# Cross attention and a mixture of 12 experts on one core: the second expert layer of 12 of 16 tiles computed only for the rows routed to each expert

## The chip, the cores and the metric

The program runs on one core of a Trainium2 chip. The metric is device time in microseconds (us) of one execution. A core has five engines that run apart from each other and wait on semaphores: TensorE (PE, matrix products into the accumulation memory PSUM), VectorE (DVE), ScalarE (ACT), GpSimd (POOL) and SyncE (SP, which here issues transfers only).

## The reference, cut to what matters

```python
x = x + xattn(layernorm(x), ctx, mask)          # (2, 1024, 256), 16 heads, 64 keys
x = x + ffn(layernorm(x))

def ffn(x):                                     # 2048 rows of 256
    xa = x @ P_w.T                              # 64 wide
    C1, C2, C3 = (route(xa, U) for U in (U1, U2, U3))   # (2048, 12), three weights not zero in a row
    h = gelu(mixture(x, C1, W1))                # W1, W2: 12 matrices of 256 x 256
    return mixture(h, C2, W2) + C3 @ b2

def route(xa, U):                               # top 3 of 12, softmax over the three
    topv, topi = top_k(xa @ U.T, 3)
    return zeros.at[rows, topi].add(softmax(topv))

def mixture(inp, C, W):
    return sum(C[:, e:e+1] * (inp @ W[e].T) for e in range(12))
```

Only three of the twelve terms of a row are not zero.

## The kernel before, in words

The 2048 rows are 16 tiles of 128 rows (T = 16), held in `x_all`. A first part runs the attention tile by tile, with the transfers and the splitting of the expert weights beside it. A second part is the two expert layers. Both compute all twelve experts for every row and let a weight of zero drop a product. Experts come in pairs: one product of a tile with a pair is 128 x 512 in one bank of PSUM, and `split_product` (L931 to L937) makes it from six matmuls, three for each half of the 256 inputs: the high parts of both operands, and each high part with the other's low part. A layer of a tile, called a slot here, is six pairs or 36 matmuls of 512 columns. There are 32 slots.

For each expert VectorE then adds weight times product to one of two running sums (`sum_pair`, L820 to L833; L827 starts a sum, L832 goes on with it), twelve for a slot, and adds the two sums (`last_sum`, L837). ScalarE makes gelu (L580), the copies of the transposed tiles and their high parts (L502, L503, L570). VectorE makes the low parts (L763, L768), the statistics of the second layernorm (L604 to L607) and its result `xf` (L626), the three best of twelve logits (`find_top`, L774 to L785) and the weights (`combine_weights`, L791 to L810). GpSimd makes the inverse deviation (`inverse_deviation2`, L366 and L368) and the exponentials (L418), and splits the weights of the third routing (`split_c3`). SyncE stores a tile once its last sum is there.

The order of the work on each engine is written out by hand, and each engine takes its own in order. In `experts(t)` layer 1 of tile t + 1 comes before layer 2 of tile t, with the next tile's logits, transposes and routing between the pairs; this is a hardware loop over t from 1 to T - 3, with straight code before and behind it. A product's bank is written again once the sums of the slot before have read it (semaphore `acc`).

## Time and profile before

| what | value |
|---|---|
| three timed runs | 409.34, 409.06, 407.38 us; median 409.06 |
| the profiled execution | 410.84 us, its span 409.1 us |
| PE busy | 393.3 us, 96% of the span |
| DVE busy | 340.5 us, 83% |
| ACT, POOL busy | 112.9 us (28%), 111.4 us (27%) |
| chain that ended last | PE 83% (line L936 alone 66%), ACT 4%, DVE 4%, issue 4% |
| PE clock | 9 tenths or more of full speed in 38 of the 40 slices of the page |

The span is the profiled part of one execution, and 1.74 us lie around it. Busy is the sum of an engine's instruction times. Matmuls are pipelined, so that a matmul of 512 columns shows about 0.39 us busy while the next starts some 0.23 us behind it; times between starts are what counts. The page's row on PE's clock is in tenths of full speed.

### The profile page before, as it was taken

Reading aid. Unit: us, or ns where it says so; the run is one execution under the profiler, and the core shown is the slowest. Engines: PE = TensorE matmul, PEld = TensorE weight load, DVE = VectorE, ACT = ScalarE, POOL = GpSimd, SP = SyncE. Lnnn points to the kernel's source line nnn. Section 1 sums busy time; section 2 is a strip of 40 time slices with the busy share of each in tenths; the row PEclk is TensorE's granted clock in tenths of the full one; section 3 lists DMA queues with packets and bytes.
Section 4 is the critical chain, followed back from the end, with each engine's and each line's share of the span. In section 5 each row is a group of like instructions: output and inputs, shape, how many; then the busy total and the mean of one; then the engine's idle time right before and its main releaser. Section 6 shows DMA issues by size and latency. Waiting matters only on the chain.

```text
span 409.1 us, 7666 instructions
## 1 busy us (share of the span) xinstructions
PE 393.3 (96%) x2132; PEld 334.5 (82%) x2132; DVE 340.5 (83%) x1038; ACT 112.9 (28%) x261; POOL 111.4 (27%) x165
## 2 busy tenths in 40 slices
PE   4889999999999999999999999999999999999996
PEld 3679889898988888888888888888888888888884
DVE  4788898998885889789898888989789898888875
ACT  2477888888932101010000100001010000100000
POOL 5264556465540211202112020211202112020200
PEclk9989999999989999999999999999999999999999
DMA  7900131322000000000000000000000000000000
GB/s 233 330 2 2 52 103 53 102 78 76 2 0 2 2 0 15 13 0 13 0 13 13 0 13 0 13 0 13 13 0 13 0 13 12 1 13 0 14 0 26
DMA packets 8613, 12.72 MB, mean 31 GB/s; under 512 B 1076, under 2 KB 5016, under 8 KB 8472
## 3 DMA queue, kind: packets, MB, share of 16 engines
q1 hardware_dynamic: 8040, 12.44, 9.2%
q10 hardware_dynamic: 560, 0.13, 0.1%
q8 instruction: 6, 0.10, 0.1%
q14 instruction: 7, 0.06, 0.0%
HBM read 10.47 MB, written 2.10 MB: 31 GB/s over the span
## 4 chain that ended last, share of the span: by engine, by line
PE 83%; ACT 4%; DVE 4%; issue 4%; POOL 2%; DMA 1%; ACTq 0%; POOLq 0%; DVEq 0%; SPq 0%
PE banks L936 66%; PE banks L978 2%; PE banks L1003 2%; PE banks L1013 2%; PE banks L988 2%; PE banks L991 1%; PE banks L1053 1%; PE banks L993 1%; ACT w_h L543 1%; DVE q_hl L637 1%; POOL w_l L377 1%; ACT prob L480 1%; PE banks L1061 1%; PE banks L1043 1%; DMA x_all<-in_x_dram 1%
## 5 line engine op out<-in xcount | busy, mean ns | idle before, releaser
L832 DVE SCALAR_TENSOR_TENSOR s_d<-banks,c_cur,s_d 128x256 f32<-128x256 f32 x165 | 72.7, 479 | 25.3 <-PE banks L936 22.2
L936 PE MATMUL banks<-w_h,xf_h 128*128 128x512 f32 x204 | 81.4, 399 | 0.0
L936 PE MATMUL banks<-w_l,xf_h 128*128 128x512 f32 x204 | 80.0, 392 | 0.0
L936 PE MATMUL banks<-w_h,xf_l 128*128 128x512 f32 x204 | 79.7, 391 | 0.0
L418 POOL TENSOR_TENSOR top_e<-euler,top_d 128x9 f32<-128x9 f32 x16 | 29.0, 1813 | 181.5 <-DVE top_d L782 181.5
L936 PE MATMUL banks<-w_h,h_h 128*128 128x512 f32 x180 | 73.0, 405 | 0.0
L936 PE MATMUL banks<-w_l,h_h 128*128 128x512 f32 x180 | 70.5, 391 | 0.0
L936 PE MATMUL banks<-w_h,h_l 128*128 128x512 f32 x180 | 70.1, 389 | 0.0
L832 DVE SCALAR_TENSOR_TENSOR sum<-banks,c_new,sum 128x256 f32<-128x256 f32 x160 | 66.3, 479 | 2.8 <-PE banks L936 2.7
L570 ACT ACTIVATE h_h<-banks 128x256 fp32r<-128x256 f32 x15 | 5.8, 386 | 156.4 <-PE banks L1061 156.4
L936 PEld LDWEIGHTS banks<-w_l,xf_h 128*128 128x128 f32 x204 | 38.4, 188 | 8.3
L936 PEld LDWEIGHTS banks<-w_h,xf_l 128*128 128x128 f32 x204 | 38.7, 190 | 7.4
L936 PEld LDWEIGHTS banks<-w_h,xf_h 128*128 128x128 f32 x204 | 38.6, 189 | 7.4
L936 PEld LDWEIGHTS banks<-w_l,h_h 128*128 128x128 f32 x180 | 33.8, 188 | 7.6
L936 PEld LDWEIGHTS banks<-w_h,h_l 128*128 128x128 f32 x180 | 33.9, 188 | 6.3
L936 PEld LDWEIGHTS banks<-w_h,h_h 128*128 128x128 f32 x180 | 33.8, 188 | 6.0
L377 POOL TENSOR_TENSOR w_l<-stage,w_h 128x1024 f32 (+1 forms) x12 | 28.7, 2391 | 32.0 <-ACT w_h L543 32.0
L1013 PE MATMUL banks<-v_ext,prob_t 128*128 128x34 f32 x256 | 30.1, 273 | 0.2 <-ACT prob_t L488 0.2
L1013 PEld LDWEIGHTS banks<-v_ext,prob_t 128*128 128x128 f32 x256 | 29.9, 192 | 0.4 <-issue 0.4
L580 ACT ACTIVATE xn_t<-xn 128x256 f32<-128x256 f32 x16 | 6.7, 420 | 77.3 <-DVE xn L837 77.3
L643 DVE TENSOR_REDUCE s_max<-banks 128x16 f32<-128x1024 f32 x16 | 19.5, 1221 | 6.3 <-PE banks L993 6.3
L488 ACT ACTIVATE prob_t<-banks 128x512 f32<-128x512 f32 x32 | 17.5, 594 | 17.1 <-PE banks L1003 17.1
(129 smaller groups left out, 628.3 us busy)
## 6 DMA issues: line engine op xcount, KB each, us to landing
stage<-in_w_t_dram SPq DMA_DIRECT2D x12, 512.0 KB, 3.6
out_dram<-x_all SPq DMA_DIRECT2D x16, 128.0 KB, 1.9
x_all<-in_x_dram SPq DMA_DIRECT2D x1, 1024.0 KB, 7.8
x_all<-in_x_dram SPq DMA_DIRECT2D x1, 768.0 KB, 8.0
mask_all<-in_mask_dram SPq DMA_DIRECT2D x2, 256.0 KB, 5.2
wk_sb<-in_wk_t_dram SPq DMA_DIRECT2D x1, 256.0 KB, 3.0
x_all<-in_x_dram SPq DMA_DIRECT2D x2, 128.0 KB, 3.8
wq_sb<-in_wq_t_dram SPq DMA_DIRECT2D x1, 256.0 KB, 4.3
```

The source lines that it names most:

```text
L377: pool.tensor_tensor(w_l[:, n, :, :], stage[:, slot, :, :], w_h[:, n, :, :].bitcast(F32), ALU.subtract).then_inc(w_split, 1)
L418: pool.tensor_tensor(top_e[:, :], euler[:, :], top_d[:, :, :].rearrange("p r k -> p (r k)"), ALU.pow).then_inc(e_ready, 1)
L488: nc.scalar.activation(prob_t[:, j:j + HP // 2, :], ps_pt[:, j:j + HP // 2, :], ACT.Copy).then_inc(pt_copied, 1)
L570: nc.scalar.activation(h_buffers(t)[0][:, :, :], ps_t, ACT.Copy).then_inc(h_hi, 1)
L580: nc.scalar.activation(h[:, :], h_in[:, :], ACT.Gelu).then_inc(h_ready, 1)
L643: dve.tensor_reduce(s_max[:, :], ps_s, AX_X, ALU.max).then_inc(s_maxed, 1)
L832: dve.scalar_tensor_tensor(out=sums[e % 2][:, :], in0=product, scalar=weights[:, e:e + 1], in1=sums[e % 2][:, :], op0=ALU.mult, op1=ALU.ad ...
L936: ins = pe.matmul(dst, a(c), b(c), start=(i == 0), stop=(i == len(terms) - 1))
L978: ins = pe.matmul(ps_q[:, m, :], wq_sb[:, c, m * P:(m + 1) * P], xn_t[:, c, :], start=(c == 0), stop=(c == C - 1))
L988: pe.matmul(banks[:, c, :].rearrange("p (h k) -> p h k", k=KEYS), ident_b[:, :], mask_bias[:, t, :].unsqueeze(1).to_broadcast([P, HPC, KEY ...
L1003: ins = pe.transpose(ps_pt[:, j, :], prob[:, 2 * j:2 * j + 2, :].rearrange("p h k -> p (h k)"), ident[:, :])
L1013: ins = pe.matmul(ps_v[:, j * 2 * VW:(j + 1) * 2 * VW], prob_t[:, j, :], v_ext[:, b, j, :], start=True, stop=True)
```

## The change: what it does

The first layer stays dense for all 16 tiles, and so does the second for the last four. For tiles 0 to 11 (S = 12) layer 2 is done from lists.

First phase, tiles 0 to 12 of layer 1 alone. For each of tiles 0 to 11 ScalarE writes gelu's result three times, each time scaled with the weight of one of the row's three choices (`weigh_h`), and GpSimd scatters the three with indirect DMAs (`send_h`) to `h_rows` in DRAM. There each expert owns a region of 13 x 128 rows. The row's place in the list comes from two small matmuls that count the rows chosen so far (`rank`) and three VectorE instructions (`rows_of`). The sums of the first pair of experts, the result of the layernorm and the copy of the logits go from VectorE to ScalarE (`first_pair`, `normalise2`, `copy_z`).

Between the phases VectorE works out a table of blocks (`table_ends`, `table_blocks`), and SyncE writes 128 rows of zeros behind the end of each of the twelve lists, at a row number that it loads from the table.

Second phase, 47 blocks of 128 rows. SyncE loads a block of `h_rows` at a row number from the table, up to eight ahead; TensorE transposes it, ScalarE and VectorE make its high and low part, TensorE multiplies it with the 256 x 256 matrix of one expert, whose offset it loads from the table, and ScalarE copies the product to a buffer that SyncE stores to `y_rows`. In the same phase the bias of tiles 0 to 11 is added to `x_all`.

Third phase, the four dense tiles as before. Beside them GpSimd fetches the results back with 36 indirect DMAs that add into `x_all`, three for each of the twelve tiles, each behind the one before it on the same tile. The loops of the expert part are now written out.

```diff
+    S = 12
+    REGION = (S + 1) * P
+    ZERO_ROW = EXPERTS * REGION
+    BLOCKS = (S * P * TOP_K + EXPERTS * (P - 1) + EXPERTS - TOP_K) // P
+    assert REGION % P == 0 and (REGION // P) * EXPERTS <= 256
...
+        h_rows = nc.dram_tensor("h_rows", (ZERO_ROW + P, D), F32)
+        y_rows = nc.dram_tensor("y_rows", (BLOCKS * P, D), F32)
...
-            def store(b, j, sums):
-                sp.wait_ge(acc, sums)
-                sp.dma_start(out_dram[:, b, j, :], x_all[:, j + b * TPB, :]).then_inc(stored, 16)
-            for b in range(BATCH):
-                with sp.Fori(0, TPB if b < BATCH - 1 else TPB - 1) as j:
-                    store(b, j, 2 * SUMS * j + (2 * SUMS * b * TPB + 3 * SUMS))
-            store(BATCH - 1, TPB - 1, 2 * SUMS * T)
+            sp.wait_ge(zeros_set, 1)
+            sp.dma_start(h_rows[ZERO_ROW:ZERO_ROW + P, :], zero_rows).then_inc(tails_set[0], 16)
+            sp.wait_ge(table, 2)
+            for e in range(EXPERTS):
+                row = sp.value_load(end_row[0:1, e:e + 1], min_val=e * REGION, max_val=e * REGION + S * P)
+                sp.dma_start(h_rows[bass.ds(row, P), :], zero_rows).then_inc(tails_set[e * ZEROS // EXPERTS], 16)
+            def load_block(j):
+                row = sp.value_load(block_row[j:j + 1, 0:1], min_val=0, max_val=ZERO_ROW)
+                if j >= LOADS:
+                    sp.wait_ge(block_t, j - LOADS + 1)
+                sp.dma_start(h_in_block[j % LOADS], h_rows[bass.ds(row, P), :]).then_inc(block_in[j % LOADS], 16)
+            sp.wait_ge(table, TABLE)
+            for i in range(2):
+                sp.wait_ge(h_sent[i], 16 * TOP_K * S // 2)
+            for i in range(ZEROS):
+                sp.wait_ge(tails_set[i], 16 * EXPERTS // ZEROS + (16 if i == 0 else 0))
+            for j in range(LOADS):
+                load_block(j)
+            for j in range(BLOCKS):
+                sp.wait_ge(block_out, j + 1)
+                sp.dma_start(y_rows[j * P:(j + 1) * P, :], y_block[j % STORES]).then_inc(y_sent[j % STORES], 16)
+                if j + LOADS < BLOCKS:
+                    load_block(j + LOADS)
+            def store(t):
+                sp.dma_start(out_dram[:, t // TPB, t % TPB, :], x_all[:, t, :]).then_inc(stored, 16)
+            for t in range(S):
+                sp.wait_ge(y_back[t], 16 * TOP_K)
+                store(t)
+            for t in range(S, T):
+                sp.wait_ge(acc, SUMS * slot2(t) + SUMS)
+                store(t)
             sp.wait_ge(stored, 16 * T)
...
+                if t >= 2:
+                    pool.wait_ge(xf_ready, t)
                 pool.tensor_tensor(rstd2[:, :], var_eps2[:, :], minus_half[:, :], ALU.pow).then_inc(rstd2_ready, 1)
+                if t >= 2:
+                    pool.wait_ge(rstd2_ready, t + 1)
+                    pool.tensor_scalar(shift2[:, :], mean_var2[:, 0:1], rstd2[:, 0:1], -1.0,
+                                       ALU.mult, ALU.mult).then_inc(shift2_ready, 1)
...
+            def send_h(t):
+                pool.wait_ge(row_set, t + 1)
+                pool.wait_ge(h_weighed, TOP_K * (t + 1))
+                for k in range(TOP_K):
+                    pool.indirect_dma_start(out=h_rows[:, :], out_offset=bass.IndirectOffsetOnAxis(h_row[:, t, k:k + 1], 0),
+                                            in_=h_w[t % 2][k], in_offset=None).then_inc(h_sent[t % 2], 16)
+            def fetch_y(t, k):
+                if k > 0:
+                    pool.wait_ge(y_back[t], 16 * k)
+                else:
+                    pool.wait_ge(y_added, t + 1)
+                pool.indirect_dma_start(out=x_all[:, t, :], out_offset=None, in_=y_rows[:, :],
+                                        in_offset=bass.IndirectOffsetOnAxis(y_row[:, t, k:k + 1], 0),
+                                        compute_op=ALU.add).then_inc(y_back[t], 16)
             exponentials(0)
             inverse_deviation2(1)
             exponentials(1)
-            split_c3(0)
-            with pool.Fori(2, T) as t:
-                inverse_deviation2(t)
-                exponentials(t)
-                split_c3(t - 1)
-            split_c3(T - 1)
+            inverse_deviation2(2)
+            for t in range(1, S + 1):
+                send_h(t - 1)
+                if t < S:
+                    inverse_deviation2(t + 2)
+                    exponentials(t + 1)
+            exponentials(S + 1)
+            for t in range(S + 1):
+                split_c3(t)
+            inverse_deviation2(S + 2)
+            fetches = [(g + i, k) for g in range(0, S, 4) for k in range(TOP_K) for i in range(4)]
+            pool.wait_ge(y_step, 4)
+            for i in range(STORES):
+                pool.wait_ge(y_sent[i], 16 * len(range(i, BLOCKS, STORES)))
+            for t, k in fetches[0:8]:
+                fetch_y(t, k)
+            split_c3(S + 1)
+            exponentials(S + 2)
+            inverse_deviation2(S + 3)
+            for t, k in fetches[8:20]:
+                fetch_y(t, k)
+            exponentials(S + 3)
+            split_c3(S + 2)
+            for t, k in fetches[20:]:
+                fetch_y(t, k)
+            split_c3(S + 3)
...
+            def weigh_h(t):
+                act.wait_ge(h_ready, t + 1)
+                if t >= 2:
+                    act.wait_ge(h_sent[t % 2], 16 * TOP_K * (t // 2))
+                for k in range(TOP_K):
+                    nc.scalar.activation(h_w[t % 2][k], h[:, :], ACT.Copy,
+                                         scale=w_all[:, t, 1, k:k + 1]).then_inc(h_weighed, 1)
+            def first_pair(t):
+                act.wait_ge(route, ROUTE_STEPS * (t + 1))
+                act.wait_ge(acc, SUMS * slot1(t))
+                act.wait_ge(pair_done, PAIRS * slot1(t) + 1)
+                for e in range(2):
+                    nc.scalar.activation(sum1[e][:, :], banks[:, BANK[0], e * D:(e + 1) * D], ACT.Copy,
+                                         scale=c_all[:, t, 0, e:e + 1]).then_inc(acc, 1)
+            def normalise2(t):
+                act.wait_ge(xft_done, t)
+                act.wait_ge(shift2_ready, t - 1)
+                nc.scalar.activation(xf[:, :], x_all[:, t, :], ACT.Identity, bias=shift2[:, 0:1],
+                                     scale=rstd2[:, 0:1]).then_inc(xf_ready, 1)
+            normalise2(2)
+            for t in range(1, S + 1):
+                gelu(t - 1)
+                weigh_h(t - 1)
+                first_pair(t)
+                copy_xf(t + 1)
+                if t < S:
+                    normalise2(t + 2)
+                copy_z(t + 1)
+            def block_high(j):
+                act.wait_ge(block_t, j + 1)
+                if j >= HT:
+                    act.wait_ge(block_done, j - HT + 1)
+                nc.scalar.activation(bt_h[j % HT], banks[:, j % HT, 0:D].rearrange("p (c t) -> p c t", c=C),
+                                     ACT.Copy).then_inc(block_hi, 1)
+            def block_copy(j):
+                act.wait_ge(block_done, j + 1)
+                if j >= STORES:
+                    act.wait_ge(y_sent[j % STORES], 16 * (j // STORES))
+                nc.scalar.activation(y_block[j % STORES], banks[:, Y_BANK[j % HT], 0:D], ACT.Copy).then_inc(block_out, 1)
+            gelu(S)
+            block_high(0)
+            block_high(1)
+            for j in range(BLOCKS):
+                if j + 2 < BLOCKS:
+                    block_high(j + 2)
+                if j % 3 == 2 and 1 <= j // 3 <= S:
+                    copy_c3t(j // 3 - 1)
+                block_copy(j)
...
+            def rows_of(t):
+                dve.wait_ge(rank_done, t + 1)
+                dve.tensor_tensor(at_rank[:, :, :], at_e[:, 1, :, :],
+                                  ps_rank.unsqueeze(2).to_broadcast([P, EXPERTS, TOP_K]), ALU.mult).then_inc(rank_used, 1)
+                if t < S - 1:
+                    with nc.allow_low_precision(reason="whole numbers up to 256"):
+                        dve.tensor_tensor(taken[:, :], taken[:, :], picked[:, :], ALU.add).then_inc(taken_set, 1)
+                dve.wait_ge(rank_used, t + 1)
+                with nc.allow_low_precision(reason="whole numbers, as integers"):
+                    dve.tensor_reduce(h_row[:, t, :], at_rank[:, :, :].rearrange("p e k -> p k e"), AX_X,
+                                      ALU.add).then_inc(row_set, 1)
...
+            for t in range(1, S + 1):
+                layer1_pairs(t, range(1, 2))
+                xf_low(t + 1)
+                layer1_pairs(t, range(2, 3))
+                if t < S:
+                    stats2(t + 2)
+                else:
+                    table_blocks()
+                layer1_pairs(t, range(3, 4))
+                if t < S:
+                    find_top(t + 1)
+                layer1_pairs(t, range(4, PAIRS))
+                if t < S:
+                    rows_of(t)
+                    if t == S - 1:
+                        table_ends()
+                    combine_weights(t + 1)
+            def block_low(j):
+                dve.wait_ge(block_hi, j + 1)
+                dve.tensor_tensor(bt_l[j % HT], banks[:, j % HT, 0:D].rearrange("p (c t) -> p c t", c=C),
+                                  bt_h[j % HT].bitcast(F32), ALU.subtract).then_inc(block_lo, 1)
+            def add_bias(t):
+                dve.wait_ge(y_done, t + 1)
+                dve.tensor_tensor(x_all[:, t, :], ps_y, x_all[:, t, :], ALU.add).then_inc(y_added, 1)
+            for j in range(BLOCKS):
+                block_low(j)
+                if j == 2:
+                    find_top(S + 1)
+                if j == 5:
+                    combine_weights(S + 1)
+                if 6 <= j < 10:
+                    rows_of_y(j - 6)
+                if j % 3 == 1 and 2 <= j // 3 <= S + 1:
+                    add_bias(j // 3 - 2)
...
+            def transpose_block(j):
+                pe.wait_ge(block_in[j % LOADS], 16 * (j // LOADS) + 16)
+                if j < HT:
+                    pe.wait_ge(acc, SUMS * S + 2 * j + 2)
+                else:
+                    pe.wait_ge(block_lo, j - HT + 1)
+                for c in range(C):
+                    ins = pe.transpose(banks[:, j % HT, c * P:(c + 1) * P], h_in_block[j % LOADS][:, c * P:(c + 1) * P],
+                                       ident[:, :])
+                ins.then_inc(block_t, 1)
+            def multiply_block(j):
+                start = pe.value_load(block_w[j:j + 1, 0:1], min_val=0, max_val=(PAIRS - 1) * 2 * C * D + D)
+                pe.wait_ge(block_lo, j + 1)
+                if j < HT:
+                    pe.wait_ge(acc, SUMS * S + 2 * (j + HT) + 2)
+                else:
+                    pe.wait_ge(block_out, j - HT + 1)
+                part = lambda w: lambda c: w[:, bass.ds(start + c * 2 * D, D)]
+                split_product(banks[:, Y_BANK[j % HT], 0:D], (lambda c: bt_h[j % HT][:, c, :], lambda c: bt_l[j % HT][:, c, :]),
+                              (part(w2_h), part(w2_l))).then_inc(block_done, 1)
+            pe.wait_ge(table, TABLE)
+            transpose_block(0)
+            transpose_block(1)
+            for j in range(BLOCKS):
+                if j + 2 < BLOCKS:
+                    transpose_block(j + 2)
+                multiply_block(j)
+                if j % 3 == 2 and 1 <= j // 3 <= S:
+                    expert_bias(j // 3 - 1)
+                if j % 3 == 1 and 1 <= j // 3 <= S:
+                    transpose_c3(j // 3 - 1)
+            pe.wait_ge(block_lo, BLOCKS)```

What SyncE does in the expert part before is this loop, run for the first eight tiles (`x_all` is a tile, `out_dram` the output):

```order
18 L318 UNCONDITIONAL_BRANCH
19 L318 ISA
20 L315 ISA [waits acc]
21 L315 DMA out_dram<-x_all 128x256
22 L318 REGISTER_ALU
23 L318 COMPARE_AND_BRANCH
```

And this is SyncE now in the second phase, two blocks of it (`prob` is a buffer of results, `bo_sb` holds the table, `stage` is a buffer of loaded blocks):

```order
99 L405 DMA y_rows<-prob 128x256 [waits block_out]
100 L391 TENSOR_LOAD bo_sb
101 L391 ISA x2
102 L394 ISA [waits block_t]
103 L394 DMA stage<-h_rows 128x256
104 L405 DMA y_rows<-prob 128x256 [waits block_out]
105 L391 TENSOR_LOAD bo_sb
106 L391 ISA x2
107 L394 ISA [waits block_t]
108 L394 DMA stage<-h_rows 128x256
```

A block has two transfers where a tile had one, and one load of a register from a table. The twelve writes of zeros stand ahead in the same form, each with its own load and one transfer.

ScalarE before, one turn of the loop of the expert part (`xn_t` is gelu's result, `h_h`, `xf_h` the high parts, `c_t` the transposed weights):

```order
150 L570 ACTIVATE h_h<-banks 128x256 [waits ht_done]
151 L574 ACTIVATE c_t<-banks 96x128 [waits c3t_done]
152 L577 REGISTER_ALU
153 L580 ACTIVATE xn_t<-xn 128x256 [waits ht_done,acc]
154 L499 REGISTER_ALU
155 L501 REGISTER_ALU [waits xft_done]
156 L502 ACTIVATE xf_t<-banks 128x256 [waits z_done]
157 L503 ACTIVATE xf_h<-banks 128x256
```

ScalarE now, one tile of the first phase (`prob_t` and `s_d` are the weighed copies, `sum_0` and `sum_1` the running sums, `xf` the result of the layernorm, `z_sb` the logits):

```order
226 L754 ACTIVATE xn_t<-xn 128x256 [waits h_weighed,acc]
227 L762 ACTIVATE prob_t<-xn_t,mask_all 128x256 [waits h_sent1,h_ready]
228 L762 ACTIVATE s_d<-xn_t,mask_all 128x256 x2
229 L771 ACTIVATE sum_0<-banks,mask_all 128x256 [waits pair_done,acc,route]
230 L771 ACTIVATE sum_1<-banks,mask_all 128x256
231 L666 ACTIVATE xf_t<-banks 128x256 [waits z_done,xft_done]
232 L667 ACTIVATE xf_h<-banks 128x256
233 L777 ACTIVATE xf<-x_all,shift,rstd 128x256 [waits shift2_ready,xft_done]
234 L673 ACTIVATE z_sb<-banks 128x36 [waits route,z_done]
```

The logits' copy stands behind the layernorm's result of the tile after, which waits for GpSimd's `shift2`.

GpSimd before, one turn of its loop:

```order
90 L366 TENSOR_TENSOR var_eps<-mean_var,eps 128x1 [waits stats2_ready]
91 L368 TENSOR_TENSOR rstd<-var_eps,minus_half 128x1 [waits var2_ready]
92 L417 ISA
93 L418 TENSOR_TENSOR top_e<-euler,top_d 128x9 [waits route]
94 L428 REGISTER_ALU [waits c_moved]
95 L429 TENSOR_TENSOR c_hlh<-c_cur,ones 128x2x12 [waits c3t_done]
96 L434 TENSOR_TENSOR c_hlh<-c_cur,c_hlh 128x12 [waits c3_hi]
```

GpSimd now, one tile of the first phase:

```order
118 L567 DMA h_rows<-prob_t,mask_all 20096x256 [waits h_weighed,row_set]
119 L567 DMA h_rows<-s_d,mask_all 20096x256 x2
120 L463 TENSOR_TENSOR var_eps<-mean_var,eps 128x1 [waits stats2_ready]
121 L467 TENSOR_TENSOR rstd<-var_eps,minus_half 128x1 [waits xf_ready,var2_ready]
122 L470 TENSOR_SCALAR shift<-mean_var,rstd 128x1 [waits rstd2_ready]
123 L546 TENSOR_TENSOR top_e<-euler,top_d 128x9 [waits route]
```

Three indirect DMAs now stand ahead of the inverse deviation, and one instruction more makes `shift2`.

## Rows read from the trace of the kernel before

**Rows 1.** Busy time by stretch: start:end, length, PE, PEld, DVE, ACT, POOL, clock, DMA

```profile
116.00:118.00 2.00, 1.03 (x5) 1.04 (x6) 1.92 (x15) 1.06 (x1) 0.35 (x1) 0.65 0.00 0
118.00:120.00 2.00, 2.00 (x7) 1.71 (x7) 1.62 (x8) 0.00 (x0) 1.92 (x3) 0.50 0.00 0
...
174.00:300.00 126.00, 126.00 (x589) 104.63 (x588) 108.97 (x374) 10.65 (x36) 21.01 (x36) 1.00 0.02 7
```

**Rows 2.** The chain that ended last: start, length, what

```profile
147.42 8.29 PE banks L936 x36
...
164.98 8.29 PE banks L936 x36
...
397.24 8.20 PE banks L936 x36
405.46 0.89 DVE s_d L832 x2
```

**Rows 3.** VectorE in order of time, start and length first, experts begin

```profile
133.99 0.20 DVE L774 COPY z_sb<-banks 128x36 f32<-128x36 f32 x1
...
137.60 0.27 DVE L810 TENSOR_REDUCE c_new<-w_at_e 128x36 f32<-128x108 f32 x1
```

**Rows 4.** VectorE in order of time, one turn of the loop

```profile
176.30 2.44 DVE L832 SCALAR_TENSOR_TENSOR sum<-banks,c_new,sum 128x256 f32<-128x256 f32 x6
178.77 0.42 DVE L837 TENSOR_TENSOR xn<-sum,sum 128x256 f32<-128x256 f32 x1
...
185.15 0.17 DVE L778 MAX8 top<-z_sb 128x8 f32<-128x12 f32 x1
...
186.01 1.74 DVE L832 SCALAR_TENSOR_TENSOR s_d<-banks,c_cur,s_d 128x256 f32<-128x256 f32 x4
...
188.34 0.27 DVE L791 TENSOR_TENSOR at_e<-top_i,iota_e 128x108 f32<-128x108 uint32 x1
...
190.02 0.43 DVE L604 BATCH_NORM_STATS2 bn<-x_all 128x6 f32 x1 [0.29 <-issue]
190.50 0.18 DVE L607 BATCH_NORM_AGGREGATE mean_var<-bn 128x2 f32<-128x6 f32 x1
...
190.81 0.88 DVE L827 TENSOR_SCALAR sum<-banks,c_new 128x256 f32<-128x256 f32 x2
```

**Rows 5.** ScalarE in order of time, same turn

```profile
179.23 0.42 ACT L580 ACTIVATE xn_t<-xn 128x256 f32<-128x256 f32 x1 [5.16 <-DVE xn L837]
179.55 0.37 ACT L502 ACTIVATE xf_t<-banks 128x256 f32<-128x256 f32 x1
```

**Rows 6.** GpSimd in order of time, same turn

```profile
185.75 1.80 POOL L418 TENSOR_TENSOR top_e<-euler,top_d 128x9 f32<-128x9 f32 x1 [11.71 <-DVE top_d L782]
...
190.75 0.19 POOL L366 TENSOR_TENSOR var_eps<-mean_var,eps 128x1 f32<-128x1 f32 x1 [1.65 <-DVE mean_var L607]
191.02 0.54 POOL L368 TENSOR_TENSOR rstd<-var_eps,minus_half 128x1 f32<-128x1 f32 x1
```

**Rows 7.** SyncE's issues of transfers in order of time

```profile
0.80 0.44 SPq L290 DMA_DIRECT2D wk_sb<-in_wk_t_dram  x1
1.30 0.45 SPq L291 DMA_DIRECT2D x_all<-in_x_dram  x1
```

**Rows 8.** Transfers by line, KB of one, median us from issue to landing

```profile
out_dram<-x_all SPq DMA_DIRECT2D x16, 128.0 KB, 1.9
```

**Rows 9.** TensorE in order of time: 256 columns at either clock, transposes

```profile
104.53 0.28 PE L936 MATMUL banks<-wo_h,a_h 128*128 128x256 f32 x1
104.64 0.28 PE L936 MATMUL banks<-wo_h,a_l 128*128 128x256 f32 x1
...
117.56 0.41 PE L936 MATMUL banks<-wo_l,a_h 128*128 128x256 f32 x1
117.77 0.41 PE L936 MATMUL banks<-wo_h,a_h 128*128 128x256 f32 x1
...
177.68 0.38 PE L1043 MATMUL banks<-ident,xf 128*128 128x128 f32 x2
177.81 0.48 PE L936 MATMUL banks<-w_h,h_h 128*128 128x512 f32 x1
```

364 lines of the change are left out of this document (267 added, 97 removed).

## The prediction

> **What bounds the kernel now.** I read the page's busy shares first (PE 96%), then the busy time by stretch: from 174 to 300 us TensorE is busy in all of 126 us at full clock, VectorE in 109 of them, ScalarE in 11 [rows 1]. The chain of waits gives the pace: the same piece of 36 matmuls comes again after 164.98 - 147.42 = 17.56 us, which is two slots, 8.78 us each [rows 2]. So each slot taken away is worth 8.78 us, as long as TensorE stays the bound, and layer 2 of twelve tiles is 12 x 8.78 = 105.4 us. The other engines' order of time then tells what bounds each new phase; in all three phases I find that it is another engine than TensorE for some or all of the time.
>
> **First phase, layer 1 of tiles 1 to 12.** It starts where the weights of tile 1 are ready, 137.9 us in the trace [rows 3]; one set of statistics comes ahead of that (0.79) and two small copies go (about 0.2 each), so 138.4.
> TensorE needs about 8.8 us for a tile. VectorE, by rows 4: ten sums at 2.47/6 = 0.41 (from 176.30 to 178.77), 4.1; the last sum and the low part, 0.42 each, 0.84; statistics 190.81 - 190.02 = 0.79; the three best 186.01 - 185.15 = 0.86; the weights 190.02 - 0.29 - 188.34 = 1.4 and one more small reduction, 0.15; three small instructions for the list places, about 0.5. Sum 8.6, as much as TensorE. What tips it are two waits that the new order makes.
> The first: the second pair waits for ScalarE's first pair, which waits for the weights that VectorE has just made. Two ScalarE instructions, 179.55 - 179.23 = 0.32 and 0.42 [rows 5], and two hand-overs of 0.04 give 0.8. Gelu and its three weighed copies stand ahead of it, but 4 x 0.32 = 1.3 fit beside the list places and the weights (2.0).
> The second: the three best of tile t + 1 wait for the copy of the logits, which stands behind the layernorm's result of tile t + 2, which waits for GpSimd. From the end of the aggregate (190.68) GpSimd has the inverse deviation at 191.56, 0.88 later [rows 4, 6]; then `shift2` about 0.25, two ScalarE instructions 0.6, hand-overs 0.1: 1.8. VectorE has one pair (0.82) in that time: a wait of 1.0. Queued behind it on VectorE are the last two pairs, whose banks TensorE needs.
> So a tile takes 8.6 + 0.8 + 1.0 = 10.4 us instead of 8.8. Eleven of them lead to 138.4 + 114.4 = 252.8, and the list ends (0.6) to 253.4.
> GpSimd's three scatters stand ahead of the inverse deviation. No row shows an indirect DMA. From below one costs an issue on SyncE, 0.5 [rows 7], from above the longest GpSimd instruction here, 1.8 [rows 6]. I take 1.2, the middle, as neither row is near. Three are 3.6 us, begun 0.6 before the weights are done, so ended 3.0 after; the statistics are ended 3.5 after. At 1.2 they hide, at 1.8 they cost about 1.5 us a tile.
>
> **Between the phases.** SyncE starts the twelve writes of zeros at about 252. Each is a load of a register, three register instructions and an issue. Issues follow each other at 1.30 - 0.80 = 0.50, and the gap in it is 0.06, which I take as the price of a register instruction (0.15 for three) [rows 7]. A register load from a table no row shows. Below it is such a gap, 0.05; above, the shortest way to memory and back, 1.9 us [rows 8]. I take 0.5, the price of the nearest thing that SyncE itself carries out, an issue. Twelve times 1.15 is 13.8; with 1.9 to land the first block is loaded from 252 + 13.8 + 1.9 = 267.7. Layer 1 of tile 12 ends at about 262, so TensorE is idle for some 8 us with the first load's landing.
> The Trainium skill ("DMA: Bandwidth & Descriptors", section "Latency and other measured facts") gives such a load a floor of about 600 ns; 0.1 us more 59 times would make the end 6 us later, some 425 us.
>
> **Second phase, 47 blocks.** TensorE: two transposes 177.81 - 177.68 = 0.13 and six matmuls of 256 columns at 0.11 to 0.12 [rows 9], 0.85 with the bias now and then. ScalarE: two instructions, 0.8. VectorE: one, 0.42. SyncE: a store 0.5, a register load 0.5, three register instructions 0.15, a load 0.5: 1.65 us a block. SyncE takes its queue in order, so prefetching eight blocks doesn't help; it is the slowest, and bounds. 47 x 1.15 + 39 x 0.5 = 73.6 to the issue of the last load: 341.3. Landing 1.9, and that block's transposes, high part, low part, product and hand-overs, 2.3: 345.5. TensorE has a register load of its own for each block, 0.5 on its sequencer, beside matmuls already queued: hidden under 1.65.
> When TensorE waits, its clock falls: after a stretch in which it was busy for half of 2 us the granted clock is 0.50, that is 1.2 GHz, and matmuls of 256 columns come every 0.21 us [rows 1, 9]. A block is then 6 x 0.21 + 0.26 = 1.5 us, still under SyncE's 1.65. It costs nothing here, but is a floor for the fast rival below. The Trainium skill warns of this ("TensorE: Matmul & The Clock Gate", section "Why this matters for your kernels": gaps between bursts take the clock back to half). By that rule no cheap register load saves more than 0.15 us a block.
>
> **Third phase.** Seven dense slots: three turns of 17.56 and 8.2 [rows 2], 60.9 us. Some 2 us more for a slow clock at its start. Beside them GpSimd has 36 fetches of 1.2, 43.2 us, and between them the exponentials of tiles 14 and 15 and `split_c3` of 13 to 15. Played through: fetches start 3 us in (the last store's 1.9 and its issue); eight take it to 12.6; exponentials (1.8) and the inverse deviation to 18.2, no later than wanted; twelve to 32.6; the exponentials of tile 15 end at 34.4, which delays its weights by about 1.2; sixteen fetches to 54.2, and only then comes `split_c3(15)`. TensorE wants its transpose 13.2 us into the third turn, at 48.3 + 1.2. It waits 5.4. Together 6.6 us; at 0.5 a fetch nothing, at 1.8 some 25. The end behind the last matmul is as before, 409.1 - 405.44 = 3.7.
>
> **The sum.** 345.5 + 60.9 + 2.0 + 6.6 + 3.7 = 418.7 us of span; with the 1.74 around it 420.4 in terms of the profiled execution (410.84). The median of the runs is 0.996 of that execution: 419 us. Set against each other: 105.4 go; 77.8 of blocks come (73.6 + 1.9 + 2.3), 18.4 of slower first phase (115.0 instead of 11 x 8.78), 5.5 of change-over (267.7 - 253.4, less the slot of tile 12), 8.6 in the third phase, and 4.7 in which TensorE's lead over VectorE at the start (it began tile 1 some 4 us before its weights were there) buys nothing more.
>
> **Rivals.**
> Cheap sequencers, faster (0.27). Register loads cost 0.15 and indirect DMAs under 0.9. The zeros land at 263.5, 47 blocks take 47 x 0.8 + 39 x 0.5 = 57, the third phase has no wait: about 391 us of span, 391 in the runs' terms; with the second wait of the first phase gone too, 382. If TensorE's half clock holds 1.5 us a block, 13 us come back, about 404. For it: the gap of 0.06 between issues says that SyncE is quick with simple things. Against: a register load has to read memory.
> Dear register loads, slower still (0.13). At 1.3 us each it is 59 x 0.8 = 47 us more: 466; at 1.9, 500. The sum crosses the 409 of before at about 0.33 us, with all else as above: from there the change is slower.
> Dear indirect DMAs, slower (0.12). At 1.8: 11 x 1.5 in the first phase and 18 in the third, about 453. For it: GpSimd builds 128 separate rows for each, and no row of this trace has anything of that kind.
> The change doesn't do what it says (0.01): the 47 blocks and their transfers all stand in the order of instructions, so that nothing speaks for it.
> My own case, SyncE bounding blocks at 1.4 to 2.0 us, has 0.47, and its own range is 405 to 440.
>
> **How the numbers follow.** A measurement of this kernel can tell about 0.5% (2 us) from no change. The fast rival gives nearly all of the chance of faster, 0.27, with a little of my own case's lower end, 0.28; its edge near 409 gives 0.05 for no change; the rest is slower, 0.67. The range of 387 to 460 leaves out the lowest of the fast rival and most of the dear register loads, one in ten each.
>
> **What would show it.** In the profile after: VectorE starts a new tile of the first phase every 10 to 11 us, with waits on ScalarE ahead of the second pair and of the three best; TensorE busy about 85% there. SyncE's issues in the second phase stand in pairs, 1.65 us a block, without waits for the blocks' semaphores; TensorE busy half of it or at half clock. In the third phase one wait of TensorE for `c3_hlh` of tile 15. Wrong would be: SyncE waiting for ScalarE's copies in the second phase (then TensorE or ScalarE bounds, and the time is 400 or less), tiles of the first phase at 9 us, or scatters that hold the inverse deviation up.

## The result, and the profile after

| | before | after |
|---|---|---|
| median of the runs | 409.2 us (407.38 to 409.44, 4 runs) | 459.76 us (458.69 to 461.17, 4 runs) |
| ratio | | 1.125, 95% interval 1.120 to 1.130 |
| span of the profiled execution | 409.1 us | 456.6 us |
| TensorE busy | 96% | 80% |

The change made the kernel 51 us slower. The prediction was 419 us, 10 us slower: the direction was right, the size was not, and the time lies at the very end of the range of 387 to 460, 20 us above the 405 to 440 of the prediction's own case. The page's shares and the by-engine line of its chain of waits say that no single engine bounds the kernel any more:

```profile
PE 366.2 (80%) x2078; PEld 303.8 (67%) x2078; DVE 278.3 (61%) x908; ACT 178.0 (39%) x439; POOL 208.9 (46%) x262
issue 23%; PE 21%; DVE 19%; POOL 17%; ACT 11%; SPq 5%; DMA 4%; POOLq 0%; DVEq 0%; ACTq 0%
```

Busy time by stretch, in the columns of [rows 1]: a piece of the first phase, the change-over, the blocks, the third phase.

```profile
174.00:262.00 88.00, 77.04 (x346) 60.42 (x347) 59.83 (x285) 29.46 (x80) 45.35 (x56) 0.94 0.11 37
264.00:283.00 19.00, 6.67 (x31) 4.98 (x31) 8.67 (x34) 3.67 (x10) 3.02 (x3) 0.78 0.33 111
300.00:350.00 50.00, 40.30 (x265) 33.20 (x265) 17.30 (x41) 22.44 (x71) 4.47 (x20) 0.97 0.51 159
364.00:457.00 93.00, 62.07 (x266) 50.28 (x264) 44.28 (x132) 7.09 (x22) 61.99 (x47) 0.84 0.43 74
```

Before, TensorE was busy in all of the 126 us of [rows 1]. Now it is idle for 12% of the first phase, two thirds of the change-over and a third of the third phase, and its granted clock is lower in each, at its lowest where it is idle most.

**First phase.** VectorE in order of time, one tile (before: [rows 4]). Between the weights of tile 5 and the three best of tile 6 stand two waits (the first row is the three best of the tile before, 11.20 us ahead of the last one, and that is the period):

```profile
193.70 0.17 DVE L1011 MAX8 top<-z_sb 128x8 f32<-128x12 f32 x1 [2.31 <-issue]
...
198.01 0.27 DVE L1047 TENSOR_REDUCE mask_all<-w_at_e 128x36 f32<-128x108 f32 x1
199.28 0.88 DVE L1074 SCALAR_TENSOR_TENSOR sum<-banks,mask_all,sum 128x256 f32<-128x256 f32 x2 [1.01 <-ACT sum L771]
...
201.65 0.18 DVE L839 BATCH_NORM_AGGREGATE mean_var<-bn 128x2 f32<-128x6 f32 x1
...
204.90 0.17 DVE L1011 MAX8 top<-z_sb 128x8 f32<-128x12 f32 x1 [2.30 <-issue]
```

GpSimd in the same tile (before: [rows 6]), where the scatters stand ahead of the inverse deviation:

```profile
199.25 1.06 POOL L567 DMA_INDIRECT h_rows<-prob_t,mask_all  x1 [3.13 <-ACT s_d L762]
200.62 0.96 POOL L567 DMA_INDIRECT h_rows<-s_d,mask_all  x1 [0.30 <-issue]
201.89 0.96 POOL L567 DMA_INDIRECT h_rows<-s_d,mask_all  x1 [0.30 <-issue]
202.87 0.20 POOL L463 TENSOR_TENSOR var_eps<-mean_var,eps 128x1 f32<-128x1 f32 x1
...
203.82 0.26 POOL L470 TENSOR_SCALAR shift<-mean_var,rstd 128x1 f32<-128x1 f32 x1
```

and ScalarE (before: [rows 5]), where the copy of the logits stands behind the normalisation:

```profile
197.57 0.90 ACT L762 ACTIVATE s_d<-xn_t,mask_all 128x256 f32<-128x256 f32 x2
...
204.18 0.60 ACT L777 ACTIVATE xf<-x_all,shift,rstd 128x256 f32<-128x256 f32 x1 [4.44 <-POOL shift L470]
204.68 0.18 ACT L673 ACTIVATE z_sb<-banks 128x36 f32<-128x36 f32 x1
```

The aggregate ends at 201.83, and GpSimd takes it up at 202.87. The wait of 2.30 is labelled "issue"; these three rows name it: the copy ends at 204.86, and VectorE goes on at 204.90.

**Change-over.** SyncE's issues (before: none of this kind; one issue is [rows 7]), with count and length of a run of them:

```profile
265.73 13.11 SPq L388 DMA_DIRECT2D h_rows<-wo_sb  x12
281.01 8.11 SPq L394 DMA_DIRECT2D stage<-h_rows  x8
289.16 0.43 SPq L405 DMA_DIRECT2D y_rows<-prob  x1
290.34 0.34 SPq L394 DMA_DIRECT2D stage<-h_rows  x1
290.72 0.43 SPq L405 DMA_DIRECT2D y_rows<-prob  x1
```

The last three are the blocks' pace, 290.72 - 289.16 = 1.56 us for a store and a load. The copies of the blocks' results, a row that sums up line 801 (count: least, median and greatest ns, first and last start), give 72.6 / 46 = 1.58:

```profile
L801 ACT ACTIVATE prob<-banks x47: 384/384/388, 288.2 to 360.8; 128x256 f32<-128x256 f32 x47
```

**Third phase.** GpSimd in order of time near its middle and end. There is nothing of the kind in the rows of before:

```profile
402.72 1.54 POOL L576 DMA_INDIRECT x_all<-y_rows,mask_all  x1 [0.30 <-issue]
404.57 1.54 POOL L576 DMA_INDIRECT x_all<-y_rows,mask_all  x1 [0.30 <-issue]
405.56 2.43 POOL L546 TENSOR_TENSOR top_e<-euler,top_d 128x9 f32<-128x9 f32 x1
...
436.52 1.55 POOL L576 DMA_INDIRECT x_all<-y_rows,mask_all  x1 [0.30 <-issue]
...
438.42 0.21 POOL L559 TENSOR_TENSOR c_hlh<-mask_all,c_hlh 128x12 f32<-128x12 f32 x1
```

One fetch starts 1.85 us behind the other. VectorE waits for the exponentials that stand behind them, and TensorE for the split of tile 15:

```profile
408.02 0.16 DVE L1030 TENSOR_REDUCE e_sum<-top_e 128x3 f32<-128x9 f32 x1 [10.54 <-POOL top_e L546]
```

```profile
438.69 0.45 PE L1407 MATMUL banks<-ident,c_hlh 128*96 128x128 f32 x1 [18.49 <-POOL c_hlh L559]
```

### The profile page after: what moved, and what is told of

The parts are those of the page before. It is cut to its first block, busy times and chain, and to the rows that moved or that the text cites. A ratio compares the mean times of both kernels' runs of the same rounds, so it can differ in the third digit from the quotient of the medians.

```text
span 456.6 us, 7680 instructions
## 1 busy us (share of the span) xinstructions
PE 366.2 (80%) x2078; PEld 303.8 (67%) x2078; DVE 278.3 (61%) x908; ACT 178.0 (39%) x439; POOL 208.9 (46%) x262
## 3 DMA queue, kind: packets, MB, share of 16 engines
q0 software_dynamic: 6912, 9.44, 10.4%
## 4 chain that ended last, share of the span: by engine, by line
issue 23%; PE 21%; DVE 19%; POOL 17%; ACT 11%; SPq 5%; DMA 4%; POOLq 0%; DVEq 0%; ACTq 0%
POOL x_all L576 11%; PE banks L1269 11%; DVE sum L1074 8%; DMA y_rows<-prob 3%; ACT prob L801 2%; ACT sum L771 2%; PE banks L1311 2%; PE banks L1336 2%; POOL top_e L546 2%; POOL w_l L480 2%; PE banks L1321 2%; SPq L387 1%; DVE q_hl L871 1%; DVE top_i L1018 1%; PE banks L1324 1%
## 5 line engine op out<-in xcount | busy, mean ns | idle before, releaser
L1074 DVE SCALAR_TENSOR_TENSOR sum<-banks,mask_all,sum 128x256 f32<-128x256 f32 x160 | 68.0, 475 | 28.0 <-ACT sum L771 14.9
L576 POOL DMA_INDIRECT x_all<-y_rows,mask_all x36 | 56.1, 1557 | 14.6 <-issue 10.4
L546 POOL TENSOR_TENSOR top_e<-euler,top_d 128x9 f32<-128x9 f32 x16 | 29.7, 1857 | 51.6 <-DVE top_d L1015 51.6
L1269 PE MATMUL banks<-w_h,h_h 128*128 128x512 f32 x120 | 52.2, 435 | 0.0
L1269 PE MATMUL banks<-w_h,xf_h 128*128 128x512 f32 x120 | 50.6, 422 | 0.0
L1269 PE MATMUL banks<-w_h,h_l 128*128 128x512 f32 x120 | 49.8, 415 | 0.0
L1269 PE MATMUL banks<-w_l,h_h 128*128 128x512 f32 x120 | 49.7, 414 | 0.0
L1269 PE MATMUL banks<-w_l,xf_h 128*128 128x512 f32 x120 | 48.5, 404 | 0.0
L1269 PE MATMUL banks<-w_h,xf_l 128*128 128x512 f32 x120 | 48.5, 404 | 0.0
L567 POOL DMA_INDIRECT h_rows<-prob_t,mask_all x24 | 24.5, 1021 | 42.8 <-ACT prob_t L762 20.4
L1269 PE MATMUL banks<-w_h,kbd_hh 128*128 x94 | 32.7, 348 | 12.7 <-ACT prob L801 9.2
L1074 DVE SCALAR_TENSOR_TENSOR s_d<-banks,mask_all,s_d 128x256 f32<-128x256 f32 x44 | 19.4, 479 | 28.2 <-PE banks L1269 27.7
L801 ACT ACTIVATE prob<-banks 128x256 f32<-128x256 f32 x47 | 18.1, 384 | 40.3 <-PE banks L1269 31.3
L777 ACT ACTIVATE xf<-x_all,shift,rstd 128x256 f32<-128x256 f32 x14 | 8.4, 602 | 54.8 <-POOL shift L470 54.8
## 6 DMA issues: line engine op xcount, KB each, us to landing
stage<-h_rows SPq DMA_DIRECT2D x47, 128.0 KB, 2.0
y_rows<-prob SPq DMA_DIRECT2D x47, 128.0 KB, 2.0
out_dram<-x_all SPq DMA_DIRECT2D x16, 128.0 KB, 2.3
h_rows<-wo_sb SPq DMA_DIRECT2D x13, 128.0 KB, 1.7
```

Of the source, the lines that this page charges most:

```text
L546: pool.tensor_tensor(top_e[:, :], euler[:, :], top_d[:, :, :].rearrange("p r k -> p (r k)"), ALU.pow).then_inc(e_ready, 1)
L567: pool.indirect_dma_start(out=h_rows[:, :], out_offset=bass.IndirectOffsetOnAxis(h_row[:, t, k:k + 1], 0), in_=h_w[t % 2][k], in_offset=No ...
L576: pool.indirect_dma_start(out=x_all[:, t, :], out_offset=None, in_=y_rows[:, :], in_offset=bass.IndirectOffsetOnAxis(y_row[:, t, k:k + 1], 0),
L801: nc.scalar.activation(y_block[j % STORES], banks[:, Y_BANK[j % HT], 0:D], ACT.Copy).then_inc(block_out, 1)
L1074: dve.scalar_tensor_tensor(out=sums[e % 2][:, :], in0=product, scalar=weights[:, e:e + 1], in1=sums[e % 2][:, :], op0=ALU.mult, op1=ALU.ad ...
L1269: ins = pe.matmul(dst, a(c), b(c), start=(i == 0), stop=(i == len(terms) - 1))
```

## The experiments

Every kernel below is the changed kernel (459.76 us) with the edit shown. The diffs give it in short. "Before" was 407 to 409 us beside each, and this difference between the rounds of runs means that 2 us or less between two kernels tell nothing. Pitch is the time from one block's result copy to the next, mean over all.

### First phase: the copy of the logits

```diff
-                if t < S:
-                    normalise2(t + 2)
                 copy_z(t + 1)
+                if t < S:
+                    normalise2(t + 2)
```

> One change in ScalarE's order in the first expert phase: the copy of the logits of tile t+1 stands ahead of the normalisation of tile t+2. Theory: the 2.30 us in which VectorE waits ahead of its MAX8 in every tile come from this copy standing behind the normalisation, which waits for the inverse deviation that GpSimd makes only between its scatters. Then that wait falls under 0.5, the tile period from 11.20 to 9.0 to 9.6 us, and the time from 460 to 436 to 443. Rival: the late inverse deviation is needed anyway and only moves the wait to TensorE's transposes or to the exponentials; then the period stays within 0.3 of 11.20 and the time within 3 us.

Measured: 435.22 us, 24.5 less. VectorE's rows:

```profile
184.18 0.17 DVE L1011 MAX8 top<-z_sb 128x8 f32<-128x12 f32 x1
...
193.00 0.17 DVE L1011 MAX8 top<-z_sb 128x8 f32<-128x12 f32 x1
```

and the busy time of the same kernel:

```profile
180.00:240.00 60.00, 60.00 (x295) 48.50 (x294) 50.91 (x240) 24.63 (x67) 39.33 (x49) 1.00 0.14 47
```

No wait stands ahead of the three best any more, and the period is 193.00 - 184.18 = 8.82, TensorE's slot of [rows 2]: a little better than the theory had it. The rival is out: GpSimd's inverse deviation still stands behind the scatters (it starts 1.04 us behind the statistics, as before), and it costs nothing here, since TensorE is busy in all of the 60 us.

### Change-over: the zeros

```diff
                 sp.dma_start(stage[...], w_dram[layer][...]).then_inc(w_in[n % RING], 16)
+                sp.dma_start(h_rows[n * REGION:n * REGION + 5 * P, :]..., zero_rows...).then_inc(tails_set, 16)
-            for e in range(EXPERTS):
-                row = sp.value_load(end_row[0:1, e:e + 1], ...)
-                sp.dma_start(h_rows[bass.ds(row, P), :], zero_rows)...
```

> The zeros that the table placed behind each expert's list between the first phase and the blocks (12 writes of 128 rows) are written early instead, at fixed rows: rows 0 to 639 of each expert's region, one write behind each of the 12 loads of expert weights, ahead of the first scatter. Theory: TensorE's 12.2 us of idle time before the blocks are SyncE's 12 issues with their register loads (13.1 us); without them the first block load is issued some 2 us behind the table, and 10 to 13 us go. Rival: the 7.9 MB of zeros delay the weight loads or the first scatters and give part of it back, so that less than 5 us goes.

Measured: 451.84 us, 7.9 less, under the expected 10 to 13. The first phase starts and ends 1.4 us later, so the early zeros cost that at most. The chain of waits shows what is late next (start, length, what):

```profile
270.46 2.42 DMA h_rows<-s_d,mask_all
272.97 0.47 SPq L390
273.95 0.36 SPq L393
```

and VectorE's last row of the table of blocks:

```profile
272.35 0.21 DVE L1173 TENSOR_SCALAR bo_sb<-wv_sb 128x1 int32<-128x1 f32 x1
```

The first load goes out at 273.95 instead of 281.01, and it could not go much earlier: the table is ready at 272.56, and tile 11's last scatter lands at 272.88. Both had been covered by the zeros. So the first load is 6.5 us behind the weights of tile 12 and not 14.9: 8.4 of the zeros' 13.1 us, less the 1.4 of the longer first part. The load is 1.4 us behind the table, as the theory wanted; its 10 to 13 us forgot that the table itself is made beside the zeros. These early zeros go to fixed rows, the first 640 of each expert's region (768 in x_best12 below), and not to the end of each list: as the edit stands, it holds only for inputs whose lists end there.

### Blocks: SyncE, TensorE or the copies

First SyncE's register loads alone:

```diff
-                row = sp.value_load(block_row[j:j + 1, 0:1], min_val=0, max_val=ZERO_ROW)
-                sp.dma_start(h_in_block[j % LOADS], h_rows[bass.ds(row, P), :])
+                sp.dma_start(h_in_block[j % LOADS], h_rows[fixed row:fixed row + P, :])
```

> SyncE's loads of the 47 blocks use fixed row numbers in place of a register loaded from the table, so the wrong rows are multiplied; the amount of data and the number of transfers stay. Theory: SyncE's own instructions set the block's 1.56 us, of which the register load is 0.65 to 0.7; without it SyncE needs 0.9 and TensorE's 1.0 to 1.2 bounds: 0.35 to 0.45 less for each of 39 blocks and 0.65 less for each of the 8 first loads, 16 to 23 us in all. Rival: the transfers (160 GB/s, 2 us of landing) or ScalarE's two copies bound the block, and less than 5 us goes.

Measured: 457.87 us, 1.9 less, pitch 1.54. The theory fell: SyncE isn't the only bound. It now waits for ScalarE's copies ahead of 44 of its 47 stores (22 before, 9.4 us in all, 37.1 now), so it has time to spare. TensorE's rows of this kernel show the other:

```profile
299.72 0.38 PE L1268 MATMUL banks<-w_h,kbd_hh 128*128 x1 [0.15 <-ACT prob L800]
...
300.54 0.38 PE L1548 MATMUL banks<-ident,stage 128*128 128x128 f32 x2
301.13 0.38 PE L1268 MATMUL banks<-w_h,kbd_hh 128*128 x1 [0.22 <-ACT prob L800]
...
302.84 0.38 PE L1268 MATMUL banks<-w_h,kbd_hh 128*128 x1 [0.41 <-ACT prob L800]
```

Ahead of each product stands a gap of 0.15 to 0.41, put down to ScalarE's `prob`. But that copy was long done, as the product needs only the one of three blocks ago. What also stands ahead of the product is TensorE's own register load. The next two kernels test this.

```diff
-                start = pe.value_load(block_w[j:j + 1, 0:1], ...)     (ahead of product j)
+                start = block_start(j + 1)                            (behind product j)
-                sp.dma_start(y_rows[j * P:(j + 1) * P, :], y_block[j % STORES])
+                act.dma_start(y_rows[j * P:(j + 2) * P, :]..., two blocks of prob_f)
```

> Two changes in the block loop together: TensorE loads the register for block j+1 right behind the product of block j (ahead of the transposes of block j+3), and the stores of the block results are issued by ScalarE, two blocks in one transfer, in place of SyncE. Theory: with fixed rows on SyncE the pitch fell only from 1.56 to about 1.47, since TensorE's own register load leaves a gap of 0.2 to 0.4 before each product; SyncE and TensorE are two bounds of nearly the same size. With both gone the pitch is 1.2 to 1.3 (ScalarE's two copies of 0.38 and half a store), 11 to 16 us less in all. Rival: the chain of ScalarE's copy, VectorE's subtraction and the three buffers bounds the loop, and less than 5 us goes, or stores on ScalarE's queue hold its copies and nothing goes.

Measured: 453.3 us, 6.5 less, pitch 1.44: half of what the theory gave.

```diff
-                return pe.value_load(block_w[j:j + 1, 0:1], ...)
+                return j // 8 * 2 * C * D + j // 4 % 2 * D
```

> The block loop of x_blocks (453.3 us, pitch 1.44), in which TensorE in addition takes its weights from fixed places in place of a register, so products use the wrong expert's weights; SyncE keeps its register loads. Theory: even behind the product TensorE's register load leaves some 0.37 ahead of the next transposes, and it is this that bounds the pitch; then it falls to 1.15 to 1.25, where ScalarE's copies and SyncE's load are next, and 9 to 13 us go from 453. Rival: the chain of transpose, ScalarE's copy, VectorE's subtraction bounds it (TensorE was seen waiting for VectorE in 16 of 40 blocks), and the pitch stays over 1.38, less than 3 us.

Measured: 445.19 us, 8.1 less than x_blocks, 1 us short of the expected range; the pitch is 57.6 / 46 = 1.25, as expected:

```profile
L799 ACT ACTIVATE prob<-banks x47: 381/383/391, 289.0 to 346.6; 128x256 f32<-128x256 f32 x47
```

So TensorE's register load costs 0.19 us a block even behind the product. With SyncE's register loads gone the block took 1.54; before, SyncE's issues filled 1.56 without a gap. These are two bounds of nearly one size, and taking one of them away shows almost nothing. SyncE's is read from its rows; no kernel took TensorE's away alone.

### Third phase: number, order and price of the fetches

```diff
-fetches = [(g + i, k) for g in range(0, S, 4) for k in range(TOP_K) for i in range(4)]
+fetches = [(g + i, k) for g in range(0, S, 4) for k in range(1) for i in range(4)]
```

> Of the 36 adding fetches only the first of three for each tile is left, 12 in all, so the outputs of two of three routed experts are left out for 12 tiles. Theory: GpSimd's 1.85 us per fetch holds up the small work that stands behind them (the weights' exponentials and the split of tile 15), 11 and 21 us of waiting. Then the third phase falls from 96 to about 67 us and the time to 428 to 434. Rival: the phase is held by TensorE's lower clock or by the dense slots themselves, and the fetches only lie beside them: then less than 5 us goes.

The small work between the fetches then stands behind the third and the seventh fetch, so that the order changes with the number. Measured: 429.16 us, 30.6 less. TensorE is busy in 57.58 of the 61 us from 364 to 425, at full clock. The rival is out.

```diff
-            for t, k in fetches[0:8]: ...
-            split_c3(S + 1); exponentials(S + 2); inverse_deviation2(S + 3)
-            for t, k in fetches[8:20]: ...
-            exponentials(S + 3); split_c3(S + 2)
-            for t, k in fetches[20:]: ...
-            split_c3(S + 3)
+            fetches[0:6]; split_c3(S + 1); exponentials(S + 2); fetches[6]; inverse_deviation2(S + 3)
+            fetches[7:12]; split_c3(S + 2); exponentials(S + 3)
+            fetches[12:16]; split_c3(S + 3); fetches[16:]
```

> All 36 fetches stay, but GpSimd's small work stands in the list where its inputs are ready: the split of tile 13 and the exponentials of tile 14 behind 6 fetches, the inverse deviation of tile 15 behind 7, the split of 14 and the exponentials of 15 behind 12, the split of 15 behind 16. Theory: the rate, not only the order, is the bound: TensorE ends some 30 us earlier, but GpSimd needs 36 x 1.85 = 66.6 and about 12 for the rest from 363.9 on, then 3.9 of landing and 2 of the store, so the end is near 449 instead of 456.6: 6 to 11 us less. Rival: order alone costs the time, and the end goes to where TensorE ends: 25 to 30 us less, as with 12 fetches.

Measured: 452.17 us, 7.6 less. VectorE's last row and GpSimd's:

```profile
425.52 0.42 DVE L1082 TENSOR_TENSOR x_all<-s_d 128x256 f32<-128x256 f32 x1
```

```profile
442.84 1.54 POOL L576 DMA_INDIRECT x_all<-y_rows,mask_all  x1 [0.30 <-issue]
```

Counted from the phase's first product (363.74 in this run), the dense tiles now end after 62.2 us, just as with twelve fetches; before this edit it was 454.2 - 360.6 = 93.6. Yet the kernel ends with the last fetch, its landing and its store. Order gives 8 us of the 31; the rest is the fetches' own time.

```diff
                 pool.indirect_dma_start(out=x_all[:, t, :], ..., in_offset=...y_row[:, t, k:k + 1]...,
-                                        compute_op=ALU.add)
+                                        )
```

> The 36 fetches write in place of adding, so the sum over a row's three experts and the residual are left out for 12 tiles; number, rows and order of the fetches stay. Theory: it is the adding that makes a fetch 1.54 us where a scatter is 1.02; then each falls to about 1.0 and the third phase ends 12 to 20 us earlier. Rival: a fetch by a list of rows costs this much with or without adding (1.54 stays), and less than 3 us goes.

Measured: 446.82 us, 12.9 less. The row of the fetches:

```profile
L576 POOL DMA_INDIRECT x_all<-y_rows,mask_all x36: 945/957/1061, 363.1 to 423.4; - x36
```

0.96 us instead of 1.55, so adding costs 0.59 us for each; without it a fetch costs what a scatter does (0.96). The pitch of plain ones is 1.26, near the 1.2 that the prediction took for all.

36 x 0.59 is 21 us, and only 12.9 came off. GpSimd, sooner done with its fetches, waits 10.1 us for the inputs of its small work, where it waited 1.9. In this kernel alone some waits are labelled "remote", VectorE's the longest (us, times, longest):

```profile
DVE s_d L1073 <- remote: 17.3, 4, 6.2
```

The wait of 6.2 stands ahead of the three best of tile 15, and with it come 3.7 of GpSimd's 10.1 us. ScalarE too copies the logits of tile 15 only at 396.11, some 5 us behind the matmuls that make them. What holds these engines up was not tested.

### How much to route, and the parts together

x_s10 changes only S (with GpSimd's small work placed between the fetches of each dense tile); x_best12 joins the copy of the logits, the early zeros, the block loop of x_blocks and the order of x_crit_first; x_best10 is the same with S = 10.

```diff
-    S = 12
+    S = 10
```

> Only the number of routed tiles goes from 12 to 10 (41 blocks, 30 fetches, 6 dense tiles), with GpSimd's small work of each dense tile placed between the fetches; none of the other repairs. Theory, from the durations of the changed kernel: two tiles less at 11.2 are 22.4, six blocks less at 1.58 are 9.5, the third phase goes from 96 to about 101, where TensorE is its bound: 459.8 - 22.4 - 9.5 + 5 = 433, between 428 and 438, still slower than before (408). Rival: the third phase is held by the fetches as before, 30 x 1.85 in the way of the dense tiles: over 445.

Measured: 432.19 us, as the sum of the durations had it (433). The rival is out: with thirty fetches, placed between the small work, TensorE is busy in 92.80 of the 94 us from 334 to 428.

> All repairs of x_best10 with 12 routed tiles as in the change (zeros written to rows 0 to 767). Theory: against 395.1 the first phase has 2 x 9.0 and the blocks 6 x 1.45 more, and GpSimd's 36 x 1.85 + 12 + landing and store (about 85 to 88 us) bound the third phase where 10 tiles needed 99.5: 395.1 + 18 + 8.7 - 13 = 409, between 405 and 413: repaired, the change as it was sized comes out even with the kernel before. Rival: the adding fetches lie beside TensorE's work as a whole, which needs only 66 us: 390 or less.

Measured: 411.16 us, ratio 1.005 (1.002 to 1.008), within the forecast: even with the kernel before, or slower by half a per cent. Its busy time in the third phase:

```profile
325.00:405.00 80.00, 57.72 (x268) 47.49 (x266) 44.48 (x132) 7.10 (x22) 62.26 (x47) 0.88 0.48 78
```

> All of these together, with 10 routed tiles in place of 12 (41 blocks, 30 fetches, 6 dense tiles): the logits' copy ahead of the normalisation, early zeros, TensorE's register loads ahead, stores on ScalarE's queue, and GpSimd's small work placed between the fetches, per dense tile. Theory: from 435.2 of the reordered copy, two tiles fewer take 2 x 9.0 and 6 x 1.56 from the first two phases, the third is bounded by TensorE again (66 + 2 x 17 = 100 us against 30 x 1.85 + some 15 on GpSimd): 412; less 12 for the blocks and 12 for the zeros: 388, between 380 and 396, so faster than the kernel without routing (408). Rival: TensorE's lower clock in the change-over and extra waits take the gains back: 400 to 412.

Measured: 395.09 us, ratio 0.970 (0.965 to 0.974): 3% faster than before, within the forecast but 7 us above its middle. Its third phase:

```profile
297.00:390.00 93.00, 92.18 (x429) 76.13 (x427) 70.82 (x224) 13.15 (x40) 60.11 (x53) 1.00 0.37 64
```

With twelve routed tiles GpSimd is the bound of this phase (62 of 80 us busy, before its gaps of 0.3), with ten TensorE is again, at full clock, and the fetches lie beside it.

```diff
-                if j + 1 < BLOCKS:
-                    start = block_start(j + 1)
+                if j % 4 == 3:
+                    starts = [block_start(i) for i in range(j + 1, min(j + 5, BLOCKS))]
```

> x_best10 with TensorE's register loads for four blocks in a row behind every fourth product. Theory: the time of a register load is mostly latency and four in a row overlap, so that the gap of 0.37 in each of 41 blocks falls to about 0.1: 8 to 11 us less than 395.1. Rival: loads run one after the other, four cost four times one and the longer gap isn't covered by a product: no gain, or up to 12 us more.

Measured: 406.46 us, 11.4 more than x_best10 (before was 1.6 higher in this round), pitch 65.5 / 40 = 1.64 instead of 1.45. TensorE's row behind one such group of four:

```profile
263.10 0.41 PE L1560 MATMUL banks<-ident,stage 128*128 128x128 f32 x2 [2.34 <-issue]
```

2.34 / 4 = 0.59 us a load. The rival was right: register loads in a row don't overlap.

## Why the prediction was wrong, point by point

The sum failed by 456.6 - 418.7 = 37.9 us of span. By its own milestones:

| milestone | predicted | measured | step, over |
|---|---|---|---|
| weights of tile 12 | 253.4 | 266.1 | 12.7 |
| first block load issued | 267.7 | 281.0 | 0.6 |
| product of the last block | 345.5 | 360.6 | 1.8 |
| end of the span | 418.7 | 456.6 | 22.8 |

**The term that failed is the price of an adding fetch.** The prediction said "no row shows an indirect DMA", set 0.5 and 1.8 as bounds and took 1.2 as the middle. It is 1.54 and a gap of 0.30, so 1.85 from start to start, above the upper bound: that row, a single GpSimd instruction, couldn't bound an instruction and the gap behind it. The mechanism was right, and was written down as the rival "dear indirect DMAs" (0.12, about 453). Played through at 1.2, TensorE waited 5.4 us for `split_c3(15)`; it waited 18.5, and VectorE 10.5 for the exponentials where 1.2 was expected. x_crit_first and x_fetch12 show that both waits go when the fetches do, or when they stand behind. One price for scatter and fetch was wrong: x_fetch_plain shows it to hold for a fetch that only writes, and the adding comes on top.

36 x 0.65 = 23 us looks like the whole 22.8, but that is partly chance. The first of the twelve fetches behind the first small work starts here and in x_fetch12, where three fetches stand ahead of that work and not eight:

```profile
384.04 1.64 POOL L576 DMA_INDIRECT x_all<-y_rows,mask_all  x1 [0.17 <-issue]
```

```profile
383.15 1.65 POOL L576 DMA_INDIRECT x_all<-y_rows,mask_all  x1 [0.16 <-issue]
```

So the first eight fetches cost 0.9 us and not 8 x 0.65: GpSimd waits there for what TensorE and VectorE make, 22.4 us into the phase even with three fetches, where the play-through had this work done at 18.2. Some 19 us of the 22.8 are the price (28 x 0.65 and the 0.9), some 4 a piece of small work whose inputs come later than it was played through. The 2.0 us for a slow clock at the phase's start were not there: from 362 to 370 us the granted clock is 1.00, and with twelve fetches the phase takes 64.6 us, which is the 60.9 and the 3.7 of the sum. The clock fell behind the waits instead, to 0.71 to 0.78 from 400 to 430 us and 0.50 from 430 to 440.

The 453 of the rival came near the result partly by luck: it had the scatters at 1.8 too, for 16.5 us in the first phase, and they cost 1.27; what made that phase longer follows.

**First phase.** Both waits were foreseen, with their causes. The one for ScalarE's pair is 1.01 (0.8 predicted), the one for the logits' copy 2.30 (1.0 predicted). VectorE's own work is 11.20 - 3.31 = 7.9, less than the 8.6 of the sum, so the period is 11.20 instead of 10.4; eleven of them are 8.8 us. "At 1.2 they hide": they don't. The first scatter starts at 199.25, 0.97 behind the weights and not 0.6 ahead, since ScalarE's three weighed copies come every 0.4 us and not every 0.32, and 0.78 us lie between the last of them (ended 198.47) and the scatter. Three pitches of 1.27 then end 1.04 us behind the statistics: scatters that hold the inverse deviation up, one of the prediction's own signs of being wrong. x_z_first shows that the whole of it hangs on one place in ScalarE's order, which the prediction had named ("with the second wait of the first phase gone too") and priced at 9 us; it is 24.5. The wait for ScalarE's pair stays there, 1.00 us, and fits beside TensorE's slot.

The other 3.9 of the 12.7 us lie at the start. The second pair of tile 1, which was to follow its weights by 0.8, comes at 142.91, 3.5 later than in the tiles behind it, and the wait for the logits' copy is 0.4 longer there (2.67). VectorE's row, then ScalarE's:

```profile
142.91 0.88 DVE L1074 SCALAR_TENSOR_TENSOR sum<-banks,mask_all,sum 128x256 f32<-128x256 f32 x2 [4.53 <-ACT sum L771]
```

```profile
138.42 0.60 ACT L777 ACTIVATE xf<-x_all,shift,rstd 128x256 f32<-128x256 f32 x1 [4.44 <-POOL shift L470]
139.03 1.28 ACT L754 ACT_TABLE_LOAD   x1
140.33 0.42 ACT L754 ACTIVATE xn_t<-xn 128x256 f32<-128x256 f32 x1
140.78 1.31 ACT L762 ACTIVATE prob_t<-xn_t,mask_all 128x256 f32<-128x256 f32 x3
142.00 0.81 ACT L771 ACTIVATE sum<-banks,mask_all 128x256 f32<-128x256 f32 x2
```

The sum had none of what stands ahead of the pair here: a normalisation that waits for GpSimd, a table load, gelu, three copies. No kernel tested it alone.

**Change-over.** Nearly right, 14.9 us against 14.3: twelve issues at 13.11 / 12 = 1.09 (1.15 predicted) and 1.70 to land (1.9). The sum had forgotten that the first block's load has a register load of its own behind the landing, 0.8 us (280.20 to 281.01).

**Blocks.** The pace was nearly right, 1.56 to 1.58 against 1.65, but the reason only half. SyncE's share is as worked out: issues are shorter (0.43 and 0.34 against 0.5 and 0.5), the register load with its instructions longer (0.75 between the store's end and the load, against 0.65). The Trainium skill ("DMA: Bandwidth & Descriptors", section "Latency and other measured facts") has a floor of about 600 ns for such a load. The 0.75 with the instructions beside it agrees with that, as do TensorE's 0.59 a load in x_best10_four, but the 6 us that it would have added were taken back by the shorter issues. Wrong was "TensorE has a register load of its own for each block, beside matmuls already queued: hidden": x_static_rows and x_static_pe show that it isn't, and that the block loop had a second bound 0.02 to 0.04 us below the first. From the first load to the last SyncE took 353.6 - 281.0 = 72.6 us (73.6 predicted), but the last product ended 7.0 behind that, not 4.2: the 1.8 in all. Wrong too was TensorE "busy half of it or at half clock": it is busy 40.30 of 50 us at a granted clock of 0.97, and the floor of 1.5 us a block at half clock did not show, since x_static_pe came to 1.25 at a clock of 0.96: gaps of 0.15 to 0.41 us, as x_static_rows has them, did not take the clock down. Cheap register loads on SyncE alone would have gained almost nothing here.

**What saved the range.** Luck. The price of the fetches and the waits of the first phase were both taken too small, with nothing to make up for them. 459.8 lies within 387 to 460 by 0.2 us, and only because the range had been stretched for a rival, dear register loads, that isn't what happened.

**What stays open.** The 3.9 us at the start weren't tried. Nor was what lies behind the "remote" waits of x_fetch_plain. A price for SyncE's register load by itself was not found by experiment either: with TensorE's bound so near, x_static_rows couldn't give it.

## What to carry to other kernels

Work that is moved off the busiest engine arrives on others as many small sequencer jobs (indirect transfers, register loads, issues): price them on the engine that carries them out, gap included, before counting what is saved, and where no row has a price, sum at both bounds. What an in-order queue holds up is decided by place: an instruction that others wait for goes ahead of one that has itself a late input, which gave 24.5 us for two swapped lines on ScalarE, and small work goes ahead of long runs of transfers that nobody waits for, which gave 7.6 us on GpSimd. Size the routed share so that the helper engine's time just fits beside the bound's: at 12 tiles GpSimd bounded the end and nothing was won, at 10 the same kernel was 3% faster than before (both with the zeros at fixed rows).

## What the runs showed of the hardware

- An indirect DMA of 128 rows of 1 KB holds GpSimd 0.96 us for a scatter or a plain fetch and 1.54 for an adding fetch, with 0.30 behind each; from its issue an adding one lands after 3.9 us, a scatter after 2.4.
- The DMA engines are not full meanwhile: while the fetches run, they are busy 43% and move 74 GB/s (364 to 457 us), less than in the block phase (159 GB/s).
- A register load on TensorE is paid between matmuls even when it stands behind a product of 0.7 us: pitch 1.44 with it, 1.25 without. Four in a row cost more, not less: pitch 1.64, with a gap of 2.34 us behind every fourth product, 0.59 a load.
- ScalarE's first gelu behind other functions cost a table load of 1.28 us.
- 7.9 MB of zeros written during the attention part cost 1.4 us there or less.
